# Attention scores with the high and low query rows of two heads in one weight tile

## What is computed

```python
# L0: x (4, 512, 1024)
w = softmax(x @ router_W.T + router_b)                 # 8 routes
out = x + 0.5 * einsum('bsn,bsnh->bsh', w, (x @ A_sum.T) @ lora_B.T)   # then nan_to_num
# L1: hidden = out, vision (4, 64, 1024)
Q = (hidden @ Wq.T + bq).reshape(4, 512, 32, 32)
K = (vision @ Wk.T + bk).reshape(4, 64, 32, 32)
V = (vision @ Wv.T + bv).reshape(4, 64, 32, 32)
scores = einsum('blhd,bvhd->bhlv', Q, K) / sqrt(32)    # masked, softmax over v
ctx = einsum('bhlv,bvhd->blhd', softmax(scores), V).reshape(4, 512, 1024)
y = hidden + ctx @ Wo.T + bo                           # then layer norm with ln_g, ln_b
```

## Time and profile before

| | us |
|---|---|
| Three runs | 681.19, 681.06, 678.75 (median 681.06) |
| Profiled execution | 679.32 |
| Span from its first to its last instruction | 677.5 |
| PE busy | 660.3 (97%) |
| DVE busy | 480.2 (71%) |
| ACT busy | 297.6 (44%) |
| POOL busy | 205.2 (30%) |

### The profile page before, as it was taken

The page is one execution under the profiler, slowest core; times in us unless marked ns, Lnnn a source line. Parts: engine busy times, 40 slices in busy tenths (PEclk is TensorE's granted clock), DMA queues, the critical chain, the costliest instruction groups (busy, mean ns, idle before and its releaser), DMA issues.

```text
span 677.5 us, 10838 instructions
## 1 busy us (share of the span) xinstructions
PE 660.3 (97%) x3687; PEld 571.1 (84%) x3687; DVE 480.2 (71%) x915; ACT 297.6 (44%) x902; POOL 205.2 (30%) x215
## 2 busy tenths in 40 slices
PE   8999989999999999999999999999999999999995
PEld 7988868888888889788878898988888988888884
DVE  5678883577556774467647788888888889888734
ACT  5452260212240132211246676666667666666511
POOL 0110001100020002000323333565665665665652
PEclk9999999999999999999999999999999999999999
DMA  8946683424774357631457994434335253423311
GB/s 301 384 131 187 173 279 141 170 70 173 256 237 167 94 190 260 204 140 47 171 130 275 351 378 142 116 104 147 114 108 176 90 170 108 144 82 110 114 73 63
DMA packets 87671, 114.67 MB, mean 169 GB/s; under 512 B 24896, under 2 KB 60352, under 8 KB 87616
## 3 DMA queue, kind: packets, MB, share of 16 engines
q1 hardware_dynamic: 87616, 113.98, 50.3%
HBM read 67.81 MB, written 46.14 MB: 168 GB/s over the span
## 4 chain that ended last, share of the span: by engine, by line
PE 87%; DVE 6%; DMA 2%; ACT 1%; SPq 1%; issue 1%; POOL 1%; DVEq 0%; ACTq 0%
PE ps L576 25%; PE ps L578 25%; PE ps L577 25%; PE ps L639 4%; PE ps L734 4%; PE ps L671 2%; DMA ctx_t<-ctxT 1%; PE ps L609 1%; DVE q_sb L906 1%; PE ps L651 1%; PE ps L610 1%; PE ps L612 1%; DMA wo_raw<-WoT 1%; DVE w_lo L804 1%; SPq L481 0%
## 5 line engine op out<-in xcount | busy, mean ns | idle before, releaser
L576 PE MATMUL ps<-wo_hi,cx_hi 128*128 128x512 f32 x256 | 104.5, 408 | 0.0
L1126 ACT ACTIVATE s_sb<-s_sb,s_min 128x64 f32<-128x64 f32 x256 | 86.2, 338 | 38.7 <-DVE s_min L932 38.7
L576 PE MATMUL ps<-act_hi,w_hi 128*128 128x512 f32 x256 | 101.6, 397 | 1.6 <-DVE q_sb L906 1.3
L578 PE MATMUL ps<-wo_hi,cx_lo 128*128 128x512 f32 x256 | 100.3, 392 | 0.0
L577 PE MATMUL ps<-wo_lo,cx_hi 128*128 128x512 f32 x256 | 100.2, 391 | 0.0
L578 PE MATMUL ps<-act_hi,w_lo 128*128 128x512 f32 x256 | 99.9, 390 | 0.0
L577 PE MATMUL ps<-act_lo,w_hi 128*128 128x512 f32 x256 | 99.9, 390 | 0.0
L1190 POOL TENSOR_TENSOR u_sb<-a_sb,w_sb 128x512 f32<-128x512 f32 x16 | 18.6, 1182 | 251.5 <-DVE w_sb L848 245.2
L1098 ACT ACTIVATE act_hi<-h_t 128x512 fp32r<-128x512 f32 x32 | 20.3, 633 | 158.3 <-DVE h_t L896 158.3
L1208 POOL TENSOR_TENSOR s_sb<-s_sb,s_min 128x256 f32<-128x256 f32 x64 | 39.4, 615 | 134.8 <-DVE s_min L932 134.8
L927 DVE SCALAR_TENSOR_TENSOR s_sb<-ps,mask_f 128x512 f32<-128x512 f32 x64 | 44.2, 691 | 48.2 <-PE ps L578 46.4
(11 more groups left out here) (117 smaller groups left out, 1525.2 us busy)
## 6 DMA issues: line engine op xcount, KB each, us to landing
q_cols<-q_sb SPq DMA_DIRECT2D x32, 512.0 KB, 3.6
qb<-q_cols SPq DMA_DIRECT2D x64, 256.0 KB, 3.5
x_sb<-xT SPq DMA_DIRECT2D x32, 256.0 KB, 3.1
h_rows<-hn_sb SPq DMA_DIRECT2D x32, 256.0 KB, 3.0
output_weights<-wo_sb SPq DMA_DIRECT2D x32, 256.0 KB, 2.8
z_sb<-h_rows SPq DMA_DIRECT2D x16, 512.0 KB, 4.4
out<-z_sb SPq DMA_DIRECT2D x15, 512.0 KB, 2.8
stage<-WvT SPq DMA_DIRECT2D x8, 512.0 KB, 5.0
```

What stands on the lines that cost most here:

```text
L576: pe.matmul(dst, lh, rh, start=(first and j == 0), stop=False)
L578: mm = pe.matmul(dst, ll, rh, start=False, stop=(last and j == n - 1))
L1126: act.activation(s_sb[c % 4][:, h, :], s_sb[c % 4][:, h, :], ACT.Exp, bias=s_min[c % 2][:, h:h + 1], scale=-1.0, accum_out=s_sum[c % 2][:, ...
```

## The change

The DRAM tensor of the queries keeps high and low parts as two separate planes. The scores of each token tile are still three matmuls, but of other shapes. The tile `k_pair` holds high key parts only, twice: for heads 2h and 2h+1 the rows 0 to 63 hold the block-diagonal keys of the two heads, and rows 64 to 127 hold the same keys again. The tile `q_pair` holds, for two heads, 64 rows of high query parts over 64 rows of low query parts. One matmul of 128 key columns gives high by high plus low by high for two heads, and two such matmuls cover the four heads. The third matmul multiplies the 128 rows of high query parts (`q_solo`) with the low keys (`k_low`), 256 columns as before. `load_keys` issues 12 DMAs instead of 8 and `load_q` issues 3 instead of 1, and the counts that PE waits for are raised to match. POOL clears the same four tiles with the first two swapped.

```diff
-    q_d = nc.dram_tensor("q_cols", (NB, KC, P, 2, TOK), F32, kind="Internal").ap()
+    q_d = nc.dram_tensor("q_cols", (NB, KC, 2, P, TOK), F32, kind="Internal").ap()
...
-        kbd = [at(f"kbd{n}", [P, HPC, KC, V], AT_B + 8192 * k, F32R) for k, n in enumerate(("_hi", "_lo"))]
+        k_pair, k_low = [at(f"k_{n}", [P, HPC, KC, V], AT_B + 8192 * k, F32R) for k, n in enumerate(("pair", "low"))]
...
-        qb = [at(f"qb{k}", [P, 2, U], AT_U_SB + 2048 * k, F32R) for k in range(4)]
+        q_pair = [at(f"q_pair{k}", [P, 2, U], AT_U_SB + 2048 * k, F32R) for k in range(4)]
+        q_solo = [at(f"q_solo{k}", [P, U], AT_WO_SB + 1024 * k, F32R) for k in range(4)]
...
             def store_q(n, place):
                 sp.wait_ge(q_copied, place + 1)
-                sp.dma_start(q_d[n // KC, n % KC].rearrange("p l t -> p (l t)"),
-                             q_sb[n % 4][:].bitcast(F32).rearrange("p l t -> p (l t)")).then_inc(q_stored[n % 4], 16)
+                sp.dma_start(q_d[n // KC, n % KC].rearrange("l p t -> p l t"), q_sb[n % 4][:].bitcast(F32)).then_inc(q_stored[n % 4], 16)
...
             def load_keys(b, half, cs):
-                for l in range(2):
-                    for j in range(HPC):
-                        rows = slice(HD * j, HD * j + HD)
-                        sp.dma_start(kbd[l][rows, j, cs, :].bitcast(F32), k_d[l, b, rows, cs, :]).then_inc(k_in[half], 16)
+                for j in range(HPC):
+                    rows = slice(HD * j, HD * j + HD)
+                    sp.dma_start(k_low[rows, j, cs, :].bitcast(F32), k_d[1, b, rows, cs, :]).then_inc(k_in[half], 16)
+                    for l in range(2):
+                        under = slice(2 * HD * l + HD * (j % 2), 2 * HD * l + HD * (j % 2) + HD)
+                        sp.dma_start(k_pair[under, j, cs, :].bitcast(F32), k_d[0, b, rows, cs, :]).then_inc(k_in[half], 16)
...
-                sp.dma_start(qb[n % 4][:].bitcast(F32), q_d[u // 2, c, :, :, U * (u % 2):U * (u % 2) + U]).then_inc(q_in[n % 4], 16)
+                cols = slice(U * (u % 2), U * (u % 2) + U)
+                for l in range(2):
+                    sp.dma_start(q_pair[n % 4][64 * l:64 * l + 64, :, :].bitcast(F32),
+                                 q_d[u // 2, c, l, :, cols].rearrange("(s p) t -> p s t", s=2)).then_inc(q_in[n % 4], 16)
+                sp.dma_start(q_solo[n % 4][:].bitcast(F32), q_d[u // 2, c, 0, :, cols]).then_inc(q_in[n % 4], 16)
...
-                    mm = three(ps_s[c % 2][:, t * HPC * V:(t + 1) * HPC * V].rearrange("p (h v) -> p h v", v=V),
-                               [(qb[n % 4][:, 0, rows], qb[n % 4][:, 1, rows], kbd[0][:, :, c, :], kbd[1][:, :, c, :])])
+                    dst = ps_s[c % 2][:, t * HPC * V:(t + 1) * HPC * V].rearrange("p (h v) -> p h v", v=V)
+
+                    for pair in range(2):
+                        heads = slice(2 * pair, 2 * pair + 2)
+                        pe.matmul(dst[:, heads, :], q_pair[n % 4][:, pair, rows], k_pair[:, heads, c, :], start=(pair == 0), stop=False)
+                    mm = pe.matmul(dst, q_solo[n % 4][:, rows], k_low[:, :, c, :], start=False, stop=True)
```

More of the change, by code:

```diff
@@ L710, in scores @@
                 b, c = n // 16, n % KC
-                pe.wait_ge(q_in[n % 4], 16 * (n // 4 + 1))
+                pe.wait_ge(q_in[n % 4], 48 * (n // 4 + 1))
                 if b == 0 or c < 4:
-                    pe.wait_ge(k_in[0], 128 * (b + 1))
+                    pe.wait_ge(k_in[0], 192 * (b + 1))
                 else:
-                    pe.wait_ge(k_in[1], 128 * b)
+                    pe.wait_ge(k_in[1], 192 * b)
                 wait(pe, s_scaled, n - 1)
@@ L1194, in zero @@
                 pool.wait_ge(h_ready, ALL)
-                for z in (kbd[0], kbd[1], vbd[0], vbd[1]):
+                for z in (k_low, k_pair, vbd[0], vbd[1]):
                     pool.memset(z[:].bitcast(F32), 0.0).then_inc(zeroed, 1)
```

## The result

| | before | changed |
|---|---|---|
| Median of 6 runs | 680.14 us | 692.87 us |
| All runs | 678.75 to 681.19 | 692.07 to 695.77 |
| Ratio | | 1.0194, 95% interval 1.0171 to 1.0216 |
| Profiled execution | 679.32 us | 693.53 us |
| Span | 677.5 us | 691.7 us |

A forecast was written before the change was run, and what follows sets the result against it. The prediction took PE's work to bound the kernel. A gain of 2.0 us from narrow matmuls and a 4.8 us later start gave +2.8 us on 680.1, so 682.9 us, with a range of 670.5 to 688.

The forecast's parts named there:

- What bounds the kernel.: Second phase: PE is busy throughout, so each 4.62 us step lasts as long as PE's work in it.
- The price of a narrow matmul.: Scores: a 128-column matmul costs 112 ns instead of 120, held up by the rate of weight loading.
- Both rivals about this price, 65 and 224 ns: Score matmuls: streaming alone sets 65 ns (670.8 us, chance 0.12), or handling as fp32 gives 224 ns (711.5 us, chance 0.13).
- The gain from it, -2.0 us.: Scores: four narrow matmuls save 32 ns a unit, over 64 units 2.0 us.
- The start.: Added SP issues delay unit 0 by 2.8 us and unit 4 by 5.5 us, a net delay of 4.8 us.
- the bound of 7.6: Start: net delay of 7.6 us if each new query DMA costs SP the 0.65 us of a present query load.
- "After that SP catches up.": Behind unit 4: SP's loads have room again, so later deliveries were costed at nothing.
- a sign that SP or the DMA engines don't keep up: After 370 us: a third PE wait on queries would show it.
- unit 52: Steady part: tightest place found, its 11.4 us from issue to use shrink to 8.5, against a landing of 3.5.
- The clock.: Units 0 to 2: a clock fall after 4.3 us idle costs nothing, unit 4's wait swallowing up to 2.7 us.
- The one in which the start isn't late: Start: unit 4's queries land earlier, so only the 2 us gain stays, 678.1 us; chance 0.05.

The follow-up runs named there:

- The two experiments on unit 14: Changed kernel without six of eight low-output-weight loads: 689.29 us; changed kernel with unit 14's queries issued ahead of the last two query stores: 690.08 us.
- the kernel with more key issues: Kernel before with 12 key DMAs in a call instead of 8, each high block in two pieces, same bytes: 683.31 us against 679.9.
- the experiment with the query issues alone: Kernel before with each unit's queries in three DMAs instead of one, same bytes: 689.05 us, ratio 1.0132.

## Why the prediction was wrong

- **What bounds the kernel.** Right. Removing 240 ns of PE's work from a step shortened it by 240 ns.
- **The price of a narrow matmul.** Nearly right. Forecast were 688 ns of scores for a unit, measured 690. In a train, narrow matmuls cost 105.5 ns each, read from the step. Both rivals about this price, 65 and 224 ns, fall.
- **The gain from it, -2.0 us.** Wrong. The scores gave back 30 ns in each steady step, but the 12 projection matmuls behind them took 2.863 us from the first's start to the next group's instead of 2.832, and the step stayed at 4.620. In the six steps with query matmuls in place of the projection the gain was there, 4.580 instead of 4.613 us. Why the projection gives it back is open: the narrow matmuls on the feed of before lose 23 of 30 ns there too, so the feed isn't needed for it. In the sum it is a term of 2 us.
- **The start.** The mechanism and unit 0's 2.8 us were right, measured 2.79. Unit 4 was forecast 5.5 us late and came 6.9 us late (8.90 - 2.00), because I priced the new query DMAs by the short key DMAs at 0.47 us and they cost 0.63. The third one for unit 4 was issued 363.86 - 353.73 - 2.00 = 8.1 us later than the single one of before, where 5.95 stood, and part of that came back by luck, since it landed after 2.3 us instead of 3.5. The net delay behind unit 5 was 6.2 us where 4.8 stood, inside the bound of 7.6.
- **"After that SP catches up."** This is the step that failed. It cost 6.0 us: 0.6 at unit 6, 3.8 at unit 14 and 1.65 for the clock behind that, less 0.1 won. PE waited for queries at units 6 and 14 too, behind 370 us, which the prediction named as a sign that SP or the DMA engines don't keep up. I named unit 52 as the tightest place with 11.4 us and didn't price unit 14, which in the kernel before had 9.0 us of room, 8.7 of them taken by its landing, while the DMA engines were full and landings took up to 10.5. The full engines and the long landing stood in the prediction, and they were the reason to look for the unit used there. SP's own lateness also moved the output weights' loads towards that unit: PE waits 0.48 of the 3.8 us for one of them. The two experiments on unit 14 show both conditions: with the same late issue and engines that aren't full its queries are on time, and issued 4.7 us earlier with full engines they no longer hold PE up.
- **The clock.** Costed at nothing. In the changed kernel the fall at unit 0 was indeed swallowed by the wait at unit 4, as argued, but that holds only where a later wait is larger; behind unit 14 none was, and in the kernel with more key issues the fall cost 2.6 us beside 1.9 of waiting.
- **The rivals.** The one in which the start isn't late fell. None had a late unit behind the start, so the range ended 4.9 us too low.

In sum: 6.2 us at the start, 0.6 at unit 6, -0.1 up to unit 13, 3.8 and 1.65 at units 14 and 15, and nothing from there on. That makes 12.2, where the medians show 12.7.

## What to carry to other kernels

Fewer columns save little once each matmul has its own weight tile: price them by the distance in a train of narrow matmuls in the trace, and ask what the same layout costs the queue that feeds it. When a change adds issues to an in-order queue, list the time from issue to use of every delivery, compare each with the landing times of its own stretch and not with the median, and start with the stretch where the DMA engines are full. Price each new wait of TensorE twice, once for the wait and once for the clock behind it, and check that a later wait really swallows it.

## What the runs showed of the hardware

- The number of runs doesn't set what a DMA issue costs SP. The query DMAs of the changed kernel, 128 runs of 1 KB each, had a median of 0.61 us over 64 partitions and 0.59 over 128; the single one of before, 256 runs over 128 partitions, had 0.52; and in the experiment with the query issues alone one with 128 runs over 128 partitions had 0.38 and those with 64 runs over 64 partitions had 0.60. The key DMAs with 32 partitions had 0.42. What sets it is open. In the stretch of full DMA engines single issues took up to 1.9 us.
- Idle stretches of PE of 3.4 to 4.3 us brought the granted clock to 1.2 GHz in each of the eight traces that had one, and a fall in the second phase cost 1.55 to 2.8 us. Behind those of 1.0 to 2.1 us it didn't fall. Between them it went either way: it fell after waits of 2.55 and 2.85 us, not after 2.46, 2.48 and 2.66, and after the gap of 2.7 to 2.8 us near 97 us in eight of fourteen executions. The last query matmul before unit 0 starts at 341.8 to 343.0 us in these eight and at 340.1 to 341.0 in the six others, so that this fall alone scatters the times of one kernel.
- The start-to-start distances of narrow and wide matmuls alternate unevenly (60, 113 and 170 ns for the three of a token tile) though their mean, 115, is what counts. A single distance would have suggested the 65 ns rival.
